# Softmax attention's stack transfers: projected rows laid dimension by dimension with the heads side by side

## The chip, the cores and the metric

The kernel runs on one core of one Trainium2 chip. The metric is the device time of one launch in microseconds (us); less is better. The median of the runs before is 2393.15 us.

## The reference

Sixteen sequences of 512 rows with 256 features pass through four residual blocks in turn: attention with a memory ("attention a"), a feed-forward block, softmax attention with rotary positions ("attention b"), and the feed-forward block again. The change is in attention b:

```python
q = jnp.einsum('kd,bsd->bsk', W_Q, in_features).reshape(B, S, H, d_k)   # 16 heads of 16 dimensions
k = jnp.einsum('kd,bsd->bsk', W_K, in_features).reshape(B, S, H, d_k)
q, k = _rope(q, THETA), _rope(k, THETA)      # mixes dimensions 2n and 2n+1 of a head
scores = jnp.einsum('bhqd,bhkd->bhqk', q, k) * scale
scores = jnp.where(causal[None, None], scores, -jnp.inf)
attn = jax.nn.softmax(scores, axis=-1)
out = jnp.einsum('bhqk,bhkd->bhqd', attn, v)
```

A score is a sum over the 16 dimensions of a head, so the order of the dimensions within a head may be chosen freely, if it is the same for q and k.

## The kernel before, in words

Four pieces of work, called lanes, run interleaved, each on its own sequence: lane 1 is attention a, lane 2 is attention b (`lane2`), F1 and F2 are the two feed-forward blocks. Every engine has its own program. On each engine the steps of the lanes are merged by `in_order` by hand-written marks (the table MARKS, L78): the step with the lowest mark is next, so each engine's order is fixed and an engine waits in place for a step that isn't ready. The 16 sequences pass through a start, a loop of 13 turns (`Fori`) that holds all four lanes, and an end. Steps are tied by semaphores alone.

Matrix products take float16 operands, with each float32 value split in a high and a low part. For attention b, lane 2 does this in each sequence:

- PB: TensorE projects q and k, 128 features (8 heads, "a half") at a time: q and k of half 0, then of half 1 (L1359). The features lie in the partitions by parity: partition r*64 + n holds feature 2n + r, so that the rotation pairs partitions n and n + 64. ScalarE copies the swapped halves (L868), VectorE and GpSimd apply cosine and sine (L1239, L709, L712), ScalarE makes the high part (L873, tile `sth`), VectorE the low part (L1244, L1248, tile `stl`). In the trace all these tiles have the name `place`.
- `stack` (L518), on the SP queue, step PB of SyncE's marks: the parts go to DRAM (`scratch`) and come back stacked, so that one product over 64 rows gives (high + low) times (high + low). For a half, four transfers write 64 partitions each to `scratch` (L531), in the natural order of the features. SP waits for their landing (L533). Then eight transfers read (L540): each fills 16 partitions (the 16 dimensions of a head) of `qst` or `kst` for 8 heads with 512 columns of float16, that is 128 KB. The fourfold stack has the rows q: high, high, low, low, and k: high, low, high, low.
- N(h), h from 0 to 15: TensorE waits for the landing of head h's half (`stacks_landed`, L1412), then computes head h's scores (`scores`, L1547, with the mask added by L1549), and VectorE takes their row maxima (L1256). The maxima are turned on TensorE (L1608) and go by small transfers within SBUF into rows 96 and 97 of `qst` (L571). NS(h) computes the scores again, transposed and shifted (L1561), ScalarE takes the exponentials (L897), PV, TP, OT and WO give the output.

Lane 1 has a `stack` of its own, with the same four writes a half, and sixteen reads of 64 KB a half (L545). Between the two stacks of lane 2, SP issues the load of lane 1's next sequence, `xa` (L552), as soon as `xa` was last used (L1060); VectorE's norm of it begins with L1024. The feed-forward blocks have UP (L1395 on TensorE, L788 and L791 on ScalarE, L649 on GpSimd) and DN (L1408). Near step N(0) of lane 2, TensorE's order is: UP steps of a feed-forward block, N(0), two more UP steps, the first of DN, N(1).

Before the lanes start there is a setup. SP loads the weights (L503), biases, the cosine and sine tables by parity (L509) and the memories (L514). VectorE waits for the weights (L952), scales and splits them; those of W_Q and W_K of attention b in `split_by_parity` (L960): 4 pieces of 128 columns a matrix, two instructions each (L967, L968). Every setup instruction of VectorE waits for the one before it (`link`).

## Time and profile before

| what | us |
|---|---|
| median of 3 runs | 2393.15 |
| lowest and highest run | 2391.18, 2405.67 |
| the profiled execution, its own time | 2384.41 |
| its span, first to last instruction | 2382.7 |

The rows further down are of the profiled execution. Its own time is 1.7 us over its span; it lies 8.7 us (0.4%) below the median. Times in the trace count from the span's start. Engines: PE is TensorE, PEld its weight loads, DVE VectorE, ACT ScalarE, POOL GpSimd, SP SyncE; a "q" behind one is its queue, where DMAs are issued and semaphores awaited. PEclk is the granted clock of TensorE as a share of 2.4 GHz. GB/s is what the core's 16 DMA engines moved in a stretch.

### The profile page before, as it was taken

The page shows a single profiled execution, that of the slowest core. Times are in us where ns is not written, and L with a number is a line of the kernel's source. Part 1 is how long each engine was busy: PE and PEld are TensorE (multiplying, and loading weights), DVE is VectorE, ACT ScalarE, POOL GpSimd, SP SyncE. Part 2 cuts the span into 40 slices and gives each one's busy share as a digit, 9 for nine tenths or more (in the row PEclk, how much of TensorE's full clock was granted, in tenths as well). Part 3 has the DMA queues.
Part 4 walks back from the last instruction along what each step waited for, and adds up shares of the span by engine and source line. Part 5 has one row for each costly group of instructions (what it writes and reads, how often), then busy time and mean ns, then how long its engine had stood idle before and what let it go on. Part 6 is the DMA issues. An engine that isn't in the chain of part 4 may idle for free. (4 is left out here: it accounts for less than half of the span.)

```text
span 2382.7 us, 53440 instructions
## 1 busy us (share of the span) xinstructions
PE 1908.6 (80%) x18306; PEld 1211.5 (51%) x18306; DVE 1604.3 (67%) x3874; ACT 1359.5 (57%) x2694; POOL 1140.0 (48%) x978
## 2 busy tenths in 40 slices
PE   0556798979888897979888797988889797888876
PEld 0334455545555554545555454555555455555443
DVE  6545776768676676868677685867667686866352
ACT  0324465756566575755666575655657575564644
POOL 0326355563635555472645546363555536363222
PEclk9668898989999998999999898999999899999999
DMA  3201414233050424224051423305142421404040
GB/s 92 54 21 42 75 42 63 64 55 73 13 93 24 63 64 63 64 30 91 8 90 38 63 64 53 74 11 90 29 63 64 63 64 25 91 13 63 1 63 10
DMA packets 125081, 126.63 MB, mean 53 GB/s; under 512 B 22800, under 2 KB 107920, under 8 KB 124816
## 3 DMA queue, kind: packets, MB, share of 16 engines
q1 hardware_dynamic: 116368, 114.58, 26.0%
q10 hardware_dynamic: 8448, 8.39, 1.1%
q8 instruction: 181, 2.97, 0.5%
q14 instruction: 84, 0.69, 0.1%
HBM read 80.43 MB, written 41.94 MB: 51 GB/s over the span
## 5 line engine op out<-in xcount | busy, mean ns | idle before, releaser
L1256 DVE TENSOR_REDUCE mxs<-bank 128x1 f32<-128x128 f32 (+3 forms) x1024 | 427.6, 480 | 167.2 <-PE bank L1549 166.5
L897 ACT ACTIVATE place<-bank 128x512 f32<-128x512 f32 (+1 forms) x768 | 348.7, 530 | 104.6 <-PE bank L1563 103.4
L659 POOL TENSOR_TENSOR place<-am,place 128x512 f16<-128x512 f32 x256 | 291.2, 1159 | 206.9 <-ACT place L803 206.9
L649 POOL TENSOR_TENSOR place<-place 128x512 f16<-128x512 f32 x256 | 300.6, 1182 | 139.9 <-ACT place L791 135.2
L1547 PE MATMUL bank<-kst,qst 96*128 96x128 f16 (+3 forms) x1024 | 258.3, 315 | 86.6 <-DMA kst<-scratch 62.9
L1408 PE MATMUL bank<-w2q,place 128*128 128x256 f16 x2048 | 248.4, 274 | 1.8 <-POOL place L649 1.0
L634 POOL TENSOR_TENSOR rstd<-ve,halfc 128x4 f32<-128x4 f32 x64 | 64.8, 1012 | 385.2 <-DVE ve L1031 385.2
L1561 PE MATMUL bank<-qst,kst 128*128 128x512 f16 (+3 forms) x1024 | 229.5, 301 | 14.9 <-DVE mxs L1256 6.7
L788 ACT ACTIVATE place<-bank,b1c 128x512 f32<-128x512 f32 x256 | 175.3, 685 | 108.4 <-PE bank L1395 88.9
L1549 PE MATMUL bank<-mask_qk,identb 128*128 128x128 bf16 x1024 | 223.2, 227 | 0.0
L687 POOL TENSOR_TENSOR place<-place 128x512 f16<-128x512 f32 x64 | 82.9, 1299 | 281.1 <-ACT place L827 260.0
L1408 PEld LDWEIGHTS bank<-w2q,place 128*128 128x128 f16 x2048 | 196.7, 98 | 36.0 <-issue 6.5
L1090 DVE SCALAR_TENSOR_TENSOR am<-bank,tri 128x512 f32<-128x512 f32 x256 | 167.3, 685 | 59.9 <-PE bank L1426 35.3
L803 ACT ACTIVATE place<-am 128x512 f16<-128x512 f32 x256 | 151.7, 628 | 93.8 <-DVE am L1090 93.8
L1395 PE MATMUL bank<-xh,w1q 128*128 128x512 f16 x512 | 168.8, 414 | 21.2 <-ACT place L788 15.2
L1547 PEld LDWEIGHTS bank<-kst,qst 96*128 96x128 f16 x1024 | 101.5, 100 | 164.6 <-DMA kst<-scratch 70.6
L1563 PE MATMUL bank<-mask_kq,identb 128*128 128x128 bf16 x1024 | 183.6, 219 | 0.0
L791 ACT ACTIVATE place<-place 128x512 f16<-128x512 f32 x256 | 161.3, 630 | 8.2
L1395 PE MATMUL bank<-xlo,w1q 128*128 128x512 f16 x512 | 165.2, 407 | 0.0
L1574 PE MATMUL bank<-place,vb 128*32 128x512 f32 (+3 forms) x2048 | 151.1, 435 | 3.2 <-ACT place L897 2.4
L666 POOL TENSOR_TENSOR place<-place 128x384 f32<-128x384 f32 x128 | 134.1, 1048 | 32.4 <-DVE place L1112 32.4
L1561 PEld LDWEIGHTS bank<-qst,kst 128*128 128x128 f16 x1024 | 101.0, 99 | 95.4 <-DVE mxs L1256 17.7
(162 smaller groups left out, 4000.5 us busy)
## 6 DMA issues: line engine op xcount, KB each, us to landing
scratch<-place SPq DMA_DIRECT2D x256, 128.0 KB, 2.4
qst<-scratch SPq DMA_DIRECT2D x256, 64.0 KB, 2.3
kst<-scratch SPq DMA_DIRECT2D x256, 64.0 KB, 2.3
qst<-scratch SPq DMA_DIRECT2D x128, 128.0 KB, 5.2
kst<-scratch SPq DMA_DIRECT2D x128, 128.0 KB, 5.8
xa<-x SPq DMA_DIRECT2D x16, 512.0 KB, 7.5
out<-xg ACTq DMA_DIRECT2D x16, 512.0 KB, 3.2
qst<-nmt SPq DMA_DIRECT2D x128, 4.0 KB, 1.8
```

The lines of the kernel that those rows point to most:

```text
L649: G.tensor_tensor(L.hl[:, m, :], L.hf[:, m % 2, :], L.hh[:, m, :], ALU.subtract).then_inc(s["hl"], 1)
L659: G.tensor_tensor(alp[:, n % 2, k, :], am[:, k, :], ahp[:, n % 2, k, :], ALU.subtract).then_inc(s["al"], 1)
L788: A.activation(L.hf[:, m % 2, :], bank_of(L, ("UP", m))[:, :], ACT.Relu, bias=b1c[:, m:m + 1]).then_inc(s["hf"], 1)
L897: A.activation(pf[h % SLOTS][:, S2_COL[k]:S2_COL[k] + S2_W[k]], bank_of(L2, ("S2", h, k))[:, 0:S2_W[k]], ACT.Exp, scale=D ** -0.5 / RS ** ...
L1090: V.scalar_tensor_tensor(am[:, k, :].rearrange("p (c s) -> p c s", c=NT), bank_of(L1, ("PR", n, k))[:, :].rearrange("p (c s) -> p c s", c= ...
L1256: V.tensor_reduce(mxs[:, g:g + 1], bank_of(L2, ("S1", n, k))[:, Q_AT[i]:Q_AT[i] + (i + 1) * P], AX, ALU.max).then_inc(s["mx"], 1)
L1395: ins = T.matmul(into[:, :], w1q[:, k, m * P:(m + 1) * P], a[:, k, :], start=(n == 0), stop=(n == 3))
L1408: ins = T.matmul(into[:, a * H:(a + 1) * H], part[:, m, cols], w2q[:, m, :], start=(m == 0 and part is L.hh), stop=(m == FT - 1 and part i ...
L1547: T.matmul(into[:, Q_AT[i]:Q_AT[i] + (i + 1) * P], L2.qst[0:STK, h, i * P:(i + 1) * P], L2.kst[0:STK, h, 0:(i + 1) * P], start=True, stop= ...
L1549: ins = T.matmul(into[:, Q_AT[i] + i * P:Q_AT[i] + (i + 1) * P], identb[:, :], mask_qk[:, :], start=False, stop=True, skip_group_check=True)
L1561: T.matmul(into[:, at:at + (NT - kt) * P], L2.kst[:, h, kt * P:(kt + 1) * P], L2.qst[:, h, kt * P:S], start=True, stop=True)
L1563: ins = T.matmul(into[:, at:at + P], identb[:, :], mask_kq[:, :], start=False, stop=True, skip_group_check=True)
```

## The change

The features of a half of attention b lie in the partitions in another order: partition r*64 + m*8 + h holds dimension 2m + r of head h, where it was dimension 2m + r at partition r*64 + h*8 + m. Read as d*8 + h, this gives 16 dimensions (the even ones first), each with its 8 heads side by side. The DRAM buffer of lane 2, `by_dim`, keeps this order, with the planes q and k apart, so that what fills a partition of `qst` or `kst` (8 heads of 512 columns, 8 KB) is one contiguous run. Four things follow:

- Writes (both lanes): two transfers a half of 128 partitions each, 256 KB, in place of four of 64 partitions, 128 KB. In lane 1 a partition's run stays 2 KB; in lane 2 it was 2 KB and becomes two of 1 KB (q and k go to different planes).
- Reads (lane 2): six a half in place of eight: two of 32 partitions fill `kst` (high and low together, 256 KB), four of 16 partitions fill `qst` (128 KB). The bytes that land are the same, 1 MB a half. Lane 1's reads are unchanged.
- Setup: the tables of cosine and sine are first copied from DRAM to DRAM in the new order, by four transfers at the head of SP's queue, and SP waits for them before it loads the tables. `split_by_parity` has twice as many instructions of half the size (64 columns), 32 in place of 16.
- The semaphores' counts follow (`bounced`, `LANDED`, `DVE_SETUP`). The marks, and so the order of steps on each engine, are the same.

```diff
--- before.py
+++ after.py
@@ -54,7 +54,7 @@
 
 
 NORM = dict(bn=4, tick=1, mv=4, ve=1, rstd=1, shift=1, xn=4, xt=2, xh=2, xl=2)
-OUTS = dict(v=2, vh=2, sh=4, sl=4, bounced=128, wo=2, xres=2)
+OUTS = dict(v=2, vh=2, sh=4, sl=4, bounced=64, wo=2, xres=2)
 FFN = dict(up=8, hf=8, hh=8, hl=8, xb=1, dn=2, xffn=2)
 PER1 = dict(
     NORM, **OUTS, xin=16, proj=4, e=4, r=4, sq=4, sk=3, skt=3,
@@ -67,7 +67,7 @@
     pv=4, ev=4, tp=4, prec=4, tb=4, ot=2, oh=2, ol=2,
 )
 PERF = dict(NORM, **FFN, store=16)
-LANDED = {1: 2 * 4 * 2 * 16, 2: 2 * 4 * 16}
+LANDED = {1: 2 * 4 * 2 * 16, 2: 6 * 16}
 
 CUT = 7
 
@@ -455,14 +455,16 @@
         prec = sb("prec", [P, 2, 16])
 
 
-        scratch = nc.dram_tensor("scratch", (2, KH, 2, P, 2, S), F16, kind="Internal").ap()
+        by_head = nc.dram_tensor("by_head", (KH, 2, P, 2, S), F16, kind="Internal").ap()
+        by_dim = nc.dram_tensor("by_dim", (KH, 2, 2, P, S), F16, kind="Internal").ap()
+        tables = nc.dram_tensor("tables", (2, 2, PAIR, S), F32, kind="Internal").ap()
         for L in (L1, L2):
             L.landed = [sem(f"landed{half}_{L.n}") for half in range(KH)]
-            L.scratch = scratch[L.n - 1]
 
         w_in = sem("w_in")
         f_in = sem("f_in")
         c_in = sem("c_in")
+        t_in = sem("t_in")
         g_in = sem("g_in")
         m_in = sem("m_in")
         pool_const = sem("pool_const")
@@ -470,7 +472,7 @@
         act_setup = sem("act_setup")
         pe_setup = sem("pe_setup")
         primed = sem("primed")
-        DVE_SETUP = 50
+        DVE_SETUP = 66
         block = ctx.enter_context(nc.Block())
 
         x_in, x_out = (t.rearrange("(b j p) f -> b p j f", b=B, p=P) for t in (x, out))
@@ -492,6 +494,10 @@
         @block.sync
         def _(sp):
             at1, at2 = marks(1, "sync"), marks(2, "sync")
+            for n, of in enumerate((cos, sin)):
+                for r in range(2):
+                    sp.dma_start(tables[n, r].rearrange("(m h) s -> m h s", h=HH8),
+                                 of.rearrange("(h m r) s -> r m h s", r=2, h=HH8)[r]).then_inc(t_in, 16)
             sp.dma_start(gates[:, 0, :], gate.broadcast_to([P, NH])).then_inc(g_in, 16)
             sp.dma_start(f_stage[:, 0:NFW].rearrange("p (k f) -> p k f", k=KH),
                          w1t.rearrange("(k p) f -> p k f", p=P)).then_inc(f_in, 16)
@@ -504,10 +510,10 @@
                              wv[:, n]).then_inc(w_in, 16)
             sp.dma_start(b1c[:, :], b1t).then_inc(c_in, 16)
             sp.dma_start(b2bc[:, :], b2.broadcast_to([P, H])).then_inc(c_in, 16)
-            for table, of in ((cost, cos), (sint, sin)):
+            sp.wait_ge(t_in, 64)
+            for n, table in enumerate((cost, sint)):
                 for r in range(2):
-                    sp.dma_start(table[r * PAIR:(r + 1) * PAIR, :],
-                                 of.rearrange("(n r) s -> r n s", r=2)[r]).then_inc(c_in, 16)
+                    sp.dma_start(table[r * PAIR:(r + 1) * PAIR, :], tables[n, r]).then_inc(c_in, 16)
             sp.wait_ge(pool_const, 1)
             for half in range(KH):
                 for h in range(HH8):
@@ -524,22 +530,26 @@
                 sp.wait_ge(s["sh"], due(L, "sh", t, 2 * half + 2))
                 sp.wait_ge(s["sl"], due(L, "sl", t, 2 * half + 2))
                 for part, src in enumerate((L.sth, L.stl)):
-                    for r in range(2):
-                        rows = slice(r * PAIR, (r + 1) * PAIR)
-                        to = L.scratch[half, part]
-                        to = to[rows] if L is L1 else to.rearrange("(n r) w s -> r n w s", r=2)[r]
-                        sp.dma_start(to, src[rows, 2 * half:2 * half + 2, :]).then_inc(s["bounced"], 16)
-
-                sp.wait_ge(s["bounced"], due(L, "bounced", t, 64 * (half + 1)))
+                    to = by_head[half, part] if L is L1 else by_dim[half, :, part].rearrange("w p s -> p w s")
+                    sp.dma_start(to, src[:, 2 * half:2 * half + 2, :]).then_inc(s["bounced"], 16)
+
+                sp.wait_ge(s["bounced"], due(L, "bounced", t, 32 * (half + 1)))
                 heads = slice(half * HH8, (half + 1) * HH8)
                 pairs = slice(half * HH8 // 2, (half + 1) * HH8 // 2)
+                if L is L2:
+                    for k in range(2):
+                        sp.dma_start(L.kst[2 * k * D:2 * (k + 1) * D, heads, :].rearrange("p h s -> p (h s)"),
+                                     by_dim[half, 1].rearrange("a (d h) s -> (a d) (h s)", h=HH8)
+                                     ).then_inc(L.landed[half], 16)
+                        for j in range(2):
+                            row = (2 * k + j) * D
+                            sp.dma_start(L.qst[row:row + D, heads, :].rearrange("p h s -> p (h s)"),
+                                         by_dim[half, 0, k].rearrange("(d h) s -> d (h s)", h=HH8)
+                                         ).then_inc(L.landed[half], 16)
+                    return
                 for k, (q_part, k_part) in enumerate(((0, 0), (0, 1), (1, 0), (1, 1))):
                     for dst, part, which in ((L.qst, q_part, 0), (L.kst, k_part, 1)):
-                        rows = L.scratch[half, part, :, which, :]
-                        if L is L2:
-                            sp.dma_start(dst[k * D:(k + 1) * D, heads, :],
-                                         rows.rearrange("(h d) s -> d h s", d=D)).then_inc(L.landed[half], 16)
-                            continue
+                        rows = by_head[half, part, :, which, :]
                         for r in range(2):
                             to = slice(r * PARTS + k * D, r * PARTS + (k + 1) * D)
                             sp.dma_start(dst[to, pairs, :], rows.rearrange("(g r d) s -> r d g s", r=2, d=D)[r]
@@ -961,11 +971,13 @@
                 for n in range(KH * H // P):
                     row, col = divmod(n * P, H)
                     at = mat % BQ * KH * H + n * P
-                    of = w_stage[mat // BQ][:, at:at + P].rearrange("p (n r) -> p r n", r=2)
-                    hi = wh[:, mat, row, col:col + P].rearrange("p (r n) -> p r n", r=2)
-                    lo = wl[:, mat, row, col:col + P].rearrange("p (r n) -> p r n", r=2)
-                    link(V.tensor_scalar(hi, of, WS, None, ALU.mult))
-                    link(V.scalar_tensor_tensor(lo, of, WS, hi, ALU.mult, ALU.subtract))
+                    for r in range(2):
+                        of = w_stage[mat // BQ][:, at:at + P].rearrange("p (h m r) -> p r m h", r=2, h=HH8)[:, r]
+                        to = slice(col + r * PAIR, col + (r + 1) * PAIR)
+                        hi = wh[:, mat, row, to].rearrange("p (m h) -> p m h", h=HH8)
+                        lo = wl[:, mat, row, to].rearrange("p (m h) -> p m h", h=HH8)
+                        link(V.tensor_scalar(hi, of, WS, None, ALU.mult))
+                        link(V.scalar_tensor_tensor(lo, of, WS, hi, ALU.mult, ALU.subtract))
 
             split_weights(0, BQ)
             split_by_parity(BQ)
```

## Rows read from the trace of the kernel before

**Rows 1.** The page: span and busy time of TensorE.

```profile
span 2382.7 us, 53440 instructions
PE 1908.6 (80%) x18306; PEld 1211.5 (51%) x18306; DVE 1604.3 (67%) x3874; ACT 1359.5 (57%) x2694; POOL 1140.0 (48%) x978
```

**Rows 2.** The chain that ended last, at sequence 14's stack: start, duration, what.

```profile
2145.18 1.41 DVE place L1244
...
2148.49 2.37 DMA scratch<-place
...
2154.07 7.66 DMA kst<-scratch
2162.17 0.32 PE bank L1547
```

**Rows 3.** Waits, PE's and SP's: total us, times, longest.

```profile
PE bank L1547 <- DMA kst<-scratch: 62.9, 16, 7.9
...
PE bank L1426 <- DMA kst<-scratch: 6.7, 2, 5.0
```
```profile
SPq L540 <- DMA scratch<-place: 106.3, 32, 6.5
```

**Rows 4.** TensorE's timeline at N(0) of four sequences: start, duration, [idle before].

```profile
262.80 0.29 PE L1547 MATMUL bank<-kst,qst 96*128 96x128 f16 x1 [7.88 <-DMA kst<-scratch]
...
528.91 0.29 PE L1547 MATMUL bank<-kst,qst 96*128 96x128 f16 x1 [2.23 <-DMA kst<-scratch]
...
1210.06 0.29 PE L1547 MATMUL bank<-kst,qst 96*128 96x128 f16 x1 [4.04 <-DMA kst<-scratch]
...
1211.52 1.06 PE L1395 MATMUL bank<-xh,w1q 128*128 128x512 f16 x2
...
1620.10 0.29 PE L1547 MATMUL bank<-kst,qst 96*128 96x128 f16 x1 [4.76 <-DMA kst<-scratch]
```

**Rows 5.** Stretches around N(0): length, busy by engine, PEclk, DMA share, GB/s.

```profile
528.70:532.10 3.40, 3.19 (x13) 1.59 (x14) 2.33 (x7) 0.23 (x1) 1.37 (x2) 0.51 0.66 230
1208.00:1214.80 6.80, 4.74 (x16) 2.17 (x17) 3.54 (x14) 1.56 (x3) 1.41 (x2) 0.50 0.80 191
...
1222.00:1275.00 53.00, 49.96 (x509) 31.78 (x509) 47.62 (x114) 35.54 (x76) 18.81 (x16) 1.00 0.27 72
```

**Rows 6.** SP's timeline, lane 2's stack of half 0.

```profile
1194.40 2.42 SPq L531 DMA_DIRECT2D scratch<-place  x4
1198.60 0.31 SPq L540 DMA_DIRECT2D qst<-scratch  x1
...
1203.27 0.40 SPq L552 DMA_DIRECT2D xa<-x  x1
```

**Rows 7.** Stretches with one kind of transfer in flight; the last column is GB/s.

```profile
1195.50:1198.20 2.70, 2.01 (x13) 1.05 (x11) 1.56 (x4) 0.60 (x2) 2.55 (x3) 1.00 0.88 194
1200.50:1209.00 8.50, 4.72 (x29) 2.37 (x26) 3.54 (x4) 7.03 (x12) 7.64 (x7) 0.94 1.17 114
1209.50:1210.50 1.00, 0.44 (x3) 0.34 (x4) 0.00 (x0) 0.00 (x0) 0.00 (x0) 0.50 1.12 354
...
4.00:5.00 1.00, 0.00 (x0) 0.00 (x0) 0.79 (x1) 0.00 (x0) 0.00 (x0) 1.00 1.03 410
```

**Rows 8.** ACT, POOL and DVE around that N(0), each from its timeline.

```profile
1207.63 0.63 ACT L791 ACTIVATE place<-place 128x512 f16<-128x512 f32 x1
```
```profile
1207.10 2.39 POOL L649 TENSOR_TENSOR place<-place 128x512 f16<-128x512 f32 x2 [0.28 <-ACT place L791]
```
```profile
1216.52 1.68 DVE L1256 TENSOR_REDUCE mxs<-bank 128x1 f32<-128x128 f32 x4 [1.98 <-PE bank L1549]
```

**Rows 9.** VectorE's timeline in the setup.

```profile
15.70 1.23 DVE L957 TENSOR_SCALAR wh<-qst 128x2048 f16<-128x2048 f32 x1 [10.90 <-DMA kst<-wall]
...
19.28 0.23 DVE L967 TENSOR_SCALAR wh<-kst 128x128 f16<-128x128 f32 x1
19.54 0.29 DVE L968 SCALAR_TENSOR_TENSOR wl<-kst,wh 128x128 f16<-128x128 f32 x1
```

## The prediction, made before the changed kernel was run

> **What bounds the kernel now.** The page comes first: TensorE is busy for 80% of the span, more than any other engine [rows 1]. An order fixed by hand adds to that the waits that stand in TensorE's own order, so the next view is the list of its waits. One of the largest is L1547, the first scores of lane 2, which waits for the landing of `kst`: 62.9 us in 16 waits, one in each sequence [rows 3]. The chain that ended last runs through the same place: the low parts (L1244), SP's writes to `scratch`, their landing, the reads, their landing, L1547 [rows 2]. So this is no idle time beside the bound. TensorE's timeline gives the single waits: 7.88 us in the first sequence, and in the three later ones shown 2.23, 4.04 and 4.76 us; the mean of the 15 after the first is (62.9 - 7.9)/15 = 3.7 us [rows 3, 4].
>
> The wait costs a second time. In the stretch 1208.0 to 1214.8 the granted clock is 0.50, that is 1.2 GHz, while from 1222 to 1275, where TensorE is hardly ever idle, it is 1.00, 2.4 GHz [rows 5]. TensorE did nothing for 4.04 us before the fall, and ran 4.74 us of work after it at half speed. In an early sequence with a wait of 2.23 us, 3.19 us of work ran so [rows 4, 5]. Between these two lie about 4 us a sequence, of which half, 2 us, would be saved at full clock.
>
> **How the path to N(0) is made up.** SP's timeline: writes issued from 1194.40, first read issued at 1198.60, N(0) starts at 1210.06 [rows 4, 6]. That is 4.2 us for the writes and 11.5 us for the reads. The stretches with one kind of transfer in flight show what sets each. Reads into 16 partitions go at 114 GB/s; writes from 64 partitions at 194; the load of `xa` into 128 partitions at 354, and its runs are 1 KB, as those of the reads are [rows 7]. Runs of 4 KB into 128 partitions (w1t and w2t, in the setup) reach 410 [rows 7]. So the rate follows how many partitions a transfer touches, and the length of a run little: 1 KB to 4 KB gives 16%, 16 to 128 partitions gives a factor of 3.
>
> **Writes.** A half is 0.52 MB: 2.7 us at 194 GB/s. With 128 partitions and runs of 1 KB I take the rate of `xa`, 354: 1.5 us. Two issues of 0.6 us (2.42/4, [rows 6]) keep ahead of that. Gain 1.2 us; bounds 0 (they stay at 194) and 1.4 (410). The `xa` row is the nearest, being the same run and partitions in the other direction.
>
> **Reads.** A half is 1.05 MB: 9.2 us at 114 GB/s. Afterwards half of the bytes (`kst`) go into 32 partitions, half (`qst`) still into 16. No row has 32 partitions; it lies between 16 (114) and 64 (194). I take 210, near the row of 64 and somewhat above, since those writes were issued one by one every 0.6 us and 128 KB in 0.6 us is 218: 2.5 us for `kst`, 4.6 us for `qst`, together 7.1, gain 2.1 us. Bounds: 0 (`kst` at 114 too) and, if the long runs lift both to 194 or more, 9.2 - 5.4 = 3.8 us. Six issues in place of eight save nothing, as data, not issue, is the limit: the eight are issued before 1203.27 [rows 6], 7 us before N(0) starts.
>
> A rule bears on this. The Trainium skill, in "SBUF — State Buffer", section "Door 1: The DMA port swizzle", says that a transfer's rate is set by the number of SBUF's 16 ports that its partitions reach: 16 partitions reach 4 (about 109 GB/s), 32 reach 8 (about 218), and 64 no more than 32. The trace agrees where it can: 114 for 16, 194 for 64 [rows 7]. By the rule's figures, as an estimate, the reads would take 2.4 + 4.8 = 7.2 us. It speaks against the "longer" in this change: a run of 8 KB gives nothing by it, and `qst` keeps its rate.
>
> N(0)'s data so lands 1.2 + 2.1 = 3.3 us earlier.
>
> **What that removes.** TensorE's readiness for N(0) doesn't depend on these transfers. The first wait, 7.88 us, keeps 4.6. The others lie between 2.2 and 4.8; less 3.3 us, those over 3.3 leave up to 1.5 us, on average 0.4 to 0.5. So 3.2 us x 15 + 3.3 = 51 us of idle time go. With waits of a few tenths to 1.5 us, I expect the clock to stay up: 2 us x 15 = 30 us. (In 1222 to 1275, with 3 us of idle time in 53, it did [rows 5].)
>
> **What is late next.** While TensorE waited (1206.0 to 1210.06), ScalarE finished its UP steps at 1208.3 and GpSimd its own at 1209.5 [rows 8]. Now two more UP steps come some 3 us sooner, and their banks and buffers with less slack; the first needs what ScalarE released before 1207. VectorE takes N(1)'s maxima at 1216.52 after a wait of 1.98 us for TensorE [rows 8], so it has room for the clock's 2 us but little over it. From 1222 on it is busy 47.6 of 53 us [rows 5]: it follows at the new time, but catches up nothing. The load of `xa` is issued at 1203.27, when `xa` is free, unchanged [rows 6]; its data stand in the queue behind the reads, and come earlier with them. I charge 0.8 us a sequence, 12 us in all; bounds 0 and 5 us a sequence (the rival below). Half 1's stack and lane 1's are not waited for in the loop, so their gain is nothing; in the start, lane 1's scores wait twice for their stacks (6.7 us, [rows 3]), which gives 1.2 us twice, 2.4.
>
> **What the setup costs.** Four copies at the head of SP's queue delay the weights, for which VectorE waits until 15.70 [rows 9]. Four issues are 2.4 us; their 0.5 MB is hidden in this if it moves at 354 GB/s, and would cost 2.2 us more at 114. I take 2.4. The wait for the copies is over long before the tables are issued, behind ten loads. The split: 8 pairs at 0.59 us (19.28 to 19.87, of which the two rows shown are 0.52 busy) become 16 pairs of half the size, each between 0.29 (no cost) and 0.59 (4.7 us more). Most of so small an instruction is fixed, so 0.48: 3.0 us more. VectorE's setup is one chain and ends last, so all 5.4 us count.
>
> **The sum.** -51 - 30 + 12 - 2.4 + 5.4 = -66 us. The profiled execution's own time, 2384.4, would become 2318. The median of the runs shown lies 8.7 us above it, so I forecast 2393.1 - 66 = 2327 us, 2.8% less.
>
> **Rivals.**
> - A. The reads gain more: the long runs lift `qst` as well. Data land 5.0 us earlier (1.2 + 3.8), every wait but the first is gone: 55 + 5 = 60 us, clock 30, charge of 12, setup 5.4, lane 1 2.4: -75, and with no charge -87. Time 2306 to 2318, say 2312. For it: nothing shows what the 16-partition reads wait for beyond their partitions. Against: 410 against 354 for longer runs [rows 7].
> - B. The reads gain nothing: 32 partitions filled in one transfer go no faster than two of 16. Then 1.2 us x 16 = 19 us of idle time, the clock falls still, setup 3 net: -16, 2377 us. That the transfers still move in runs of 1 KB, so that the change does not do what it says, would leave `kst` its 32 partitions, and is my forecast unless this rival holds as well.
> - C. The wait goes, another takes its place: ScalarE, GpSimd or VectorE holds N(1), UP or DN so that half of the 81 us come back, -40 + 3 = -37: 2356 us. For it: the row of POOL ends 3.5 us after TensorE went idle. Against: VectorE's wait of 1.98 us for TensorE [rows 8].
> - D. Slower. A 16-partition transfer is now 16 runs of 8 KB, one for each DMA engine, where it was 128 runs. If so few and long runs keep an engine from overlapping one with the next, the rate falls. It decides from where the reads take over 9.2 + 1.2 = 10.4 us, 101 GB/s. With a quarter of the rate lost (86 GB/s, 12.2 us) N(0) comes 1.8 us later: 29 us + 3 = +32, 2425 us. Against: 4 KB runs are the fastest seen [rows 7].
>
> **Chances.** Forecast 0.50, A 0.20, B 0.15, C 0.10, D 0.05. Apart from D all are below the time before; about 1% (24 us) is what a measurement can tell from no change. The forecast, A and C lie beyond it and make 0.80 together, a little of B's range reaches it: faster 0.81; same 0.14, from B and the mild end of D; slower 0.05. The range runs from A with no charge (2306), with a little for an unseen gain, to a weak B: 2300 to 2380.
>
> **What would show it.** L1547's wait for `kst` on TensorE falls from 62.9 us to some 10 to 12, most of it in the first sequence. From the first write's issue to the first read's it is about 3 us (4.2 before), and from there to the landing about 9 (11.5 before). The rate in the reads swings between some 110 and 200 GB/s with the kind of transfer. After N(0) the granted clock is 1.00, and L1395's pairs take 0.59 us where they took 1.06 [rows 4]. The setup ends 5 us later. It is wrong if the reads' total stays at 9 us of data, if the clock still falls after N(0), or if L1408, L1395 or the scores of N(1) to N(3) show new waits of over 1 us.

## The result, and the profile after

| what | us |
|---|---|
| before, median of 4 runs (lowest, highest) | 2392.3 (2391.2, 2405.7) |
| after, median of 4 runs (lowest, highest) | 2300.7 (2298.3, 2303.0) |
| ratio, with its 95% interval | 0.9605 [0.9569, 0.9641] |
| the profiled execution of after, its own time, its span | 2303.0, 2301.3 |

By the medians the change gains 91.6 us, 3.8%; the ratio compares means and gives 4.0%. The forecast was 66 us and 2327, with a range of 2300 to 2380. The median after lies at its lowest end, and 0.9605 of the 2393.15 us on record is 2298.6, just below it: more was gained than the forecast allowed for. The page of after, span and engines, then the queue that fetches instructions (packets, MB, share):

```profile
span 2301.3 us, 53268 instructions
...
PE 1904.0 (83%) x18306; PEld 1207.5 (52%) x18306; DVE 1617.6 (70%) x3890; ACT 1361.3 (59%) x2694; POOL 1140.6 (50%) x978
...
q14 instruction: 23, 0.19, 0.0%
```

The same queue on the page of before:

```profile
q14 instruction: 84, 0.69, 0.1%
```

TensorE is busy 4.6 us less than before [rows 1], its idle time falls from 474.1 to 397.3 us (span less busy). So almost all of the profiled difference is idle time, though the forecast had 30 us of it in the clock. TensorE's waits after, total, times and longest; the new number of L1547 is L1559, that of L1443 is L1455:

```profile
PE bank L1455 <- DVE am L1102: 46.1, 26, 3.2
...
PE bank L1407 <- ACT place L798: 14.5, 33, 2.2
PE bank L1559 <- DMA qst<-by_dim: 7.9, 6, 4.0
```

and the row of before that answers to the first:

```profile
PE bank L1443 <- DVE am L1090: 78.6, 26, 4.9
```

The wait for the stack falls from 62.9 us [rows 3] to 7.9 (forecast: 10 to 12). Of the 7.9, 3.98 are in the first sequence, and the next five wait 0.45 to 1.21 us each; after those, the data land 0.1 to 1.9 us before N(0) starts. But a second wait falls as well, by 32.5 us, of which the prediction had nothing: lane 1's products that wait for VectorE's `am`.

**At N(0)**, it goes by the plan. SP's timeline, then TensorE's:

```profile
1292.94 0.91 SPq L534 DMA_DIRECT2D by_dim<-place  x2
1295.88 0.33 SPq L541 DMA_DIRECT2D kst<-by_dim  x1
...
1303.24 0.40 SPq L562 DMA_DIRECT2D xa<-x  x1
```
```profile
1305.84 0.22 PE L1559 MATMUL bank<-kst,qst 96*128 96x128 f16 x1
...
1306.62 0.59 PE L1407 MATMUL bank<-xh,w1q 128*128 128x512 f16 x2
...
1309.08 1.27 PE L1420 MATMUL bank<-w2q,place 128*128 128x256 f16 x10 [0.40 <-ACT place L798]
```

First write to first read is 2.94 us where it was 4.20 [rows 6]. N(0) starts without idle time before it, 9.96 us after the first read's issue (11.46 before). The pair L1407 takes 0.59 us, where L1395 took 1.06 at half clock [rows 4]. The windows of after (length, busy by engine, PEclk, DMA share, GB/s), for the writes, the reads, and the reads' end with the load of `xa`:

```profile
1293.80:1295.40 1.60, 1.60 (x16) 1.31 (x14) 1.46 (x3) 0.60 (x2) 1.46 (x3) 1.00 0.95 323
1297.50:1303.20 5.70, 5.62 (x38) 3.38 (x36) 2.29 (x5) 4.77 (x9) 5.55 (x5) 1.00 0.90 164
1303.50:1310.20 6.70, 5.87 (x35) 2.91 (x36) 4.79 (x15) 6.37 (x11) 5.55 (x6) 1.00 0.59 179
```

Writes go at 323 GB/s (194 before), reads at 164 (114 before, [rows 7]), and the clock is full. The reads' packets run from 1296.8 to 1303.1: 1.05 MB in 6.3 us. This is one of the faster stacks. Over half 0 of all 16 sequences the data take 6.2 to 8.2 us, in the median 6.9. From the issue of the first read to the last landing it is 8.8 us in the median (8.1 to 9.9), and was 11.5 (10.9 to 12.2) before.

**At the end of a turn of the loop** VectorE had a pause between two instructions, with nothing it waited for ("issue"). There are 12 such pauses in before, 32.0 us in all; this one is 2.60. Before, then after:

```profile
1307.51 0.28 DVE L1121 TENSOR_TENSOR xlo<-bank,xh 128x128 f16<-128x128 f32 x1
1310.39 1.41 DVE L1024 BATCH_NORM_STATS2 stats<-xb 128x6 f32<-128x256 f32 x4 [2.60 <-issue]
```
```profile
1272.30 0.28 DVE L1133 TENSOR_TENSOR xlo<-bank,xh 128x128 f16<-128x128 f32 x1
1272.70 1.40 DVE L1036 BATCH_NORM_STATS2 stats<-xb 128x6 f32<-128x256 f32 x4
```

The pause is gone in every turn. TensorE's `L1443` waited right behind it, and the clock stood at half. TensorE's row of before, then the half-clock stretch at that place before and after:

```profile
1313.80 0.63 PE L1443 MATMUL bank<-bmh,place 64*128 64x272 f16 x4 [4.65 <-DVE am L1090]
```
```profile
1310.40:1317.20 6.80, 3.40 (x36) 2.74 (x36) 5.15 (x23) 2.08 (x4) 2.03 (x2) 0.50 0.01 2
```
```profile
1274.50:1284.70 10.20, 6.78 (x46) 4.30 (x47) 7.30 (x23) 4.62 (x9) 4.29 (x4) 0.51 0.01 2
```

This also says why the busy time hardly fell: half clock at N(0) is gone except in the first sequence, but the stretch at the loop's end is longer and holds 6.78 us of work in place of 3.40. Over the span the half-clock time goes from 344 to 295 us.

**The setup** costs more than forecast. VectorE after:

```profile
21.92 1.23 DVE L967 TENSOR_SCALAR wh<-qst 128x2048 f16<-128x2048 f32 x1 [17.12 <-DMA kst<-wall]
...
25.51 0.21 DVE L979 TENSOR_SCALAR wh<-kst 128x64 f16<-128x64 f32 x1
25.75 0.26 DVE L980 SCALAR_TENSOR_TENSOR wl<-kst,wh 128x64 f16<-128x64 f32 x1
26.05 0.21 DVE L979 TENSOR_SCALAR wh<-kst 128x64 f16<-128x64 f32 x1
```

The weights come 6.2 us later (21.92 against 15.70, [rows 9]); a pair takes 0.54 us (25.51 to 26.05), 16 of them 8.6, against 8 of 0.59, 4.7.

### The profile page after: what moved, and what is told of

Its sections match the earlier page's. It is cut to its first block and busy times, and to the rows that moved or that the text cites. A ratio compares the mean times of both kernels' runs of the same rounds, so it can differ in the third digit from the quotient of the medians.

```text
span 2301.3 us, 53268 instructions
## 1 busy us (share of the span) xinstructions
PE 1904.0 (83%) x18306; PEld 1207.5 (52%) x18306; DVE 1617.6 (70%) x3890; ACT 1361.3 (59%) x2694; POOL 1140.6 (50%) x978
## 5 line engine op out<-in xcount | busy, mean ns | idle before, releaser
L1559 PE MATMUL bank<-kst,qst 96*128 96x128 f16 (+3 forms) x1024 | 250.8, 306 | 33.5 <-DVE mxs L1268 16.9
L1561 PE MATMUL bank<-mask_qk,identb 128*128 128x128 bf16 x1024 | 218.2, 222 | 0.0
L1407 PE MATMUL bank<-xh,w1q 128*128 128x512 f16 x512 | 157.8, 391 | 21.5 <-ACT place L798 14.5
L1407 PE MATMUL bank<-xlo,w1q 128*128 128x512 f16 x512 | 156.1, 387 | 0.0
L1559 PEld LDWEIGHTS bank<-kst,qst 96*128 96x128 f16 x1024 | 99.6, 98 | 107.5 <-DVE mxs L1268 37.1
L818 ACT ACTIVATE xh<-bank 128x128 f16<-128x128 f32 x128 | 35.6, 278 | 201.5 <-PE bank L1482 199.5
```

What stands on the lines that cost most here:

```text
L1407: ins = T.matmul(into[:, :], w1q[:, k, m * P:(m + 1) * P], a[:, k, :], start=(n == 0), stop=(n == 3))
L1559: T.matmul(into[:, Q_AT[i]:Q_AT[i] + (i + 1) * P], L2.qst[0:STK, h, i * P:(i + 1) * P], L2.kst[0:STK, h, 0:(i + 1) * P], start=True, stop= ...
L1561: ins = T.matmul(into[:, Q_AT[i] + i * P:Q_AT[i] + (i + 1) * P], identb[:, :], mask_qk[:, :], start=False, stop=True, skip_group_check=True)
```

## The experiments

Two theories of the 91.6 us stand against each other. F: some 30 us are no effect of the transfers; the 16 added setup instructions shifted VectorE's code behind them, and with it the pause at the loop's end. The rival: all comes from the transfers, the pause went because the phase of the loop changed. On the transfers' side, theory P says that the number of partitions sets the rate, and the length of a run does not.

### e1 and e2: the code's place alone

e1 is the kernel before with 16 instructions more in VectorE's setup, e2 the kernel after with 112 more. They touch no transfer.

```diff
-        DVE_SETUP = 50
+        DVE_SETUP = 66
...
+            for _ in range(16):
+                link(V.memset(L1.tick[:, :], 0.0))
             split_weights(0, BQ)
```

> The kernel before with 16 more tiny instructions in VectorE's setup (they write a tile that is written again later), nothing else. Theory F (placement of code): in the kernel before VectorE stands 2.6 us at the end of every turn of the loop, with nothing in the profile that it waits for, and queue 14 fetches instructions in every turn; the changed kernel has neither, since its 16 more setup instructions moved the loop's code. By F this kernel loses the 2.6 us too: a period of 133.5 to 134 us in place of 136.3, queue 14 at some 25 packets in place of 84, time 2360 to 2368 us. Rival (the stall went because the stacks land earlier, or because SP issues less): period 136.3, 84 packets, time 2394 us, 2 us of setup more.

Measured: 2365.3 us, ratio 0.9849 [0.982, 0.9878], against 2397.7 for before, measured beside it: 32 us gained by adding work. e1's instruction queue, its waits and VectorE's loop end (a turn of its own):

```profile
q14 instruction: 24, 0.20, 0.0%
```
```profile
PE bank L1549 <- DMA kst<-scratch: 65.2, 16, 7.4
...
PE bank L1445 <- DVE am L1092: 44.8, 26, 3.2
```
```profile
1163.85 0.28 DVE L1123 TENSOR_TENSOR xlo<-bank,xh 128x128 f16<-128x128 f32 x1
1164.25 1.40 DVE L1026 BATCH_NORM_STATS2 stats<-xb 128x6 f32<-128x256 f32 x4
```

The wait for the stack stays (65.2), that for `am` falls to the value of after. The stretch at half clock at the loop's end grows as it does in after, with the transfers untouched, and TensorE's busy time rises from 1908.6 to 1925.1 us: the clock takes back part of what the pause gave.

```profile
1300.30:1310.50 10.20, 7.70 (x48) 4.63 (x49) 6.45 (x21) 5.47 (x11) 3.72 (x5) 0.50 0.01 2
```

> The changed kernel with 112 more tiny instructions in VectorE's setup. A packet of queue 14 is 8 KB, so if an instruction is 64 bytes (an estimate), 16 + 112 = 128 bring the loop's code back to where it lay in the kernel before, relative to such a block. Theory F: the stall of about 2.6 us a turn and the fetches in each turn come back, the period goes from 129.7 to about 132.3 us, time 2300 + 34 + 10 (setup) = 2344 us. Rival (the stall went for another reason): period 129.7, time 2310 us, only the setup longer.

Measured: 2343.3 us, 0.9768 [0.9743, 0.9793]; the pause is back, with the packets and the wait:

```profile
q14 instruction: 84, 0.69, 0.1%
```
```profile
PE bank L1457 <- DVE am L1104: 76.8, 24, 4.9
```
```profile
1301.98 0.28 DVE L1135 TENSOR_TENSOR xlo<-bank,xh 128x128 f16<-128x128 f32 x1
1304.90 1.40 DVE L1038 BATCH_NORM_STATS2 stats<-xb 128x6 f32<-128x256 f32 x4 [2.65 <-issue]
```

Of its 42.6 us over after, 15.7 are the added instructions (N(0) of the first sequence comes so much later) and 27 the loop. The pause can be taken away and put back without touching a transfer: the rival falls.

The trace also shows what stands in the pause. This is the instruction queue's row for the stretch 1308.20 to 1309.00 of before, inside the pause that begins at 1307.79:

```profile
q14 instruction: 1, 0.01, 2.5%
```

The packet starts 0.72 us after the pause begins and has ended 1.56 us before VectorE's next instruction. All 12 pauses of before hold one such packet, and so do the 12 of e2 and the 12 of e7 (0.7 to 1.0 us into the pause). From one pause to the next the queue has 5 packets; 12 turns of 5 are the 60 that go or come. In e1 from 500 to 2100 us and in after from 500 to 2040, that is in the loop, it has none.

### e3 and e4: partitions or runs

e3 reads `kst` in 16-partition transfers again (eight reads a half), in the order `qst`, `kst` as before; all else is as after. e4 keeps the six reads and pads a row of `by_dim`, so that its runs are 1 KB.

```diff
# e3
-                        sp.dma_start(L.kst[2 * k * D:2 * (k + 1) * D, heads, :].rearrange("p h s -> p (h s)"),
-                                     by_dim[half, 1].rearrange("a (d h) s -> (a d) (h s)", h=HH8)
...
+                            for dst, which, part in ((L.qst, 0, k), (L.kst, 1, j)):
+                                sp.dma_start(dst[row:row + D, heads, :].rearrange("p h s -> p (h s)"),
+                                             by_dim[half, which, part].rearrange("(d h) s -> d (h s)", h=HH8)
# e4
-        by_dim = nc.dram_tensor("by_dim", (KH, 2, 2, P, S), F16, kind="Internal").ap()
+        by_dim = nc.dram_tensor("by_dim", (KH, 2, 2, P, S + 64), F16, kind="Internal").ap()[:, :, :, :, 0:S]
...
```

> The changed kernel with the reads of kst cut in two, so that all eight fill 16 partitions, still with runs of 8 KB, in the order q, k, q, k as before. Theory P (the rate is set by the partitions that a transfer reaches): 114 GB/s again, from the first read's issue to the landing about 11 us where the changed kernel has under 8.5, a wait of 2 to 3 us at N(0) in every sequence, the clock at half after N(0), time 2300 + 45 to 60 = 2345 to 2360 us. Theory L (long runs made the reads faster): landing after some 8 us, no wait at N(0) in the loop, time 2300 to 2306 us.

> The changed kernel with each row of 512 columns padded in DRAM by 64 columns, so that the same six reads into the same 32 and 16 partitions move in runs of 1 KB and not of 8 KB. Theory P: as the changed kernel, data of the reads in 6 to 7.2 us, no wait at N(0) in the loop, 2300 us plus or minus 4. Theory L: back to 9 us of data, a wait of 1 to 2 us at N(0), 2315 to 2345 us.

Measured: e3 2318.1 us, 0.9671 [0.9632, 0.9709]; e4 2305.5, 0.9613 [0.9596, 0.963]. The reads of e3, then of e4:

```profile
1314.00:1321.00 7.00, 6.21 (x40) 3.51 (x39) 3.54 (x4) 6.36 (x12) 6.59 (x5) 1.00 1.00 113
```
```profile
1170.20:1176.50 6.30, 5.71 (x39) 3.48 (x38) 2.90 (x5) 5.30 (x10) 6.15 (x5) 1.00 1.05 164
```

P holds in this: runs of 8 KB into 16 partitions go at 113 GB/s, no faster than runs of 1 KB did before, and runs of 1 KB go at 164 in the reads of after. e3 can't say whether the 32 partitions or the order does it, for e3 also brings back the order of before, in which `qst` and `kst` are filled for the same 16 partitions one behind the other; that is e7's question. The longer runs bring the last landing 0.8 us sooner (8.8 us after the first read's issue in after, 9.7 in e4), but little of that reaches the time: at most the 5 us between after and e4, which were measured apart and whose intervals overlap. Rival D ends here. e3's last landing comes 11.1 us after the first read's issue, as expected, but its time is only 17 us over after's, where 45 to 60 were expected. Its waits at N(0) came back, 29.5 us in all, but short, and in 13 of 16 sequences the clock stayed up:

```profile
1323.10 0.23 PE L1557 MATMUL bank<-kst,qst 96*128 96x128 f16 x1 [1.24 <-DMA kst<-by_dim]
...
1323.89 0.59 PE L1405 MATMUL bank<-xh,w1q 128*128 128x512 f16 x2
```

### e5 and e8: four writes again, alone and with e3

```diff
                 for part, src in enumerate((L.sth, L.stl)):
...
+                    for r in range(2):
+                        rows = slice(r * PAIR, (r + 1) * PAIR)
...
+                        sp.dma_start(to, src[rows, 2 * half:2 * half + 2, :]).then_inc(s["bounced"], 16)
```

> The changed kernel with the writes of both lanes cut in two again, four of 64 partitions. Theory P: from the first write's issue to the first read's 4.2 us again, where it is 2.9. The data for N(0) land 1.3 us later; in the loop of the changed kernel they land some 2 us before TensorE is ready, so nothing of this shows but in the first sequence (1.3 us) and for lane 1's first stacks: 2301 to 2305 us. Rival (the writes are worth their 1.3 us in every sequence): 2300 + 20 = 2320 us.

> The changed kernel with both kinds of transfer cut as they were, four writes of 64 partitions and eight reads of 16: what is left of the change is the order of the rows, runs of 8 KB, the longer setup, and the place of VectorE's code. Theory P: transfers as in the kernel before (4.2 us and some 11 us), so the time of the kernel before without VectorE's stall (2365 us) plus the setup's 10: 2370 to 2378 us. Rival (long runs still give part): 2335 to 2360 us. From e3, whose landing took 11.1 to 11.4 us with two writes, 2345 to 2355 could also come out if the 1.3 us of the writes count fully (1.3 x 2 x 15 with the clock).

Measured: e5 2321.0 us, 0.9685 [0.9654, 0.9717]; e8 2372.0, 0.9911 [0.988, 0.9943], the 2370 to 2378 of its theory P. In e5 the writes take 4.48 us to the first read, and N(0) waits in every sequence:

```profile
1305.63 2.67 SPq L536 DMA_DIRECT2D by_dim<-place  x4
1310.11 0.33 SPq L543 DMA_DIRECT2D kst<-by_dim  x1
```
```profile
PE bank L1561 <- DMA qst<-by_dim: 27.8, 16, 6.1
```

Theory P of the expectation, 2301 to 2305 us, is wrong here. The writes are 1.5 us later and the reads' last landing 0.5 us more (9.3 us after the first issue, 8.8 in after), 2.0 in all; after has 0.1 to 1.9 us to spare in ten of its sequences and none in the other six. Undoing the writes costs 20 us, the 32 partitions 17, but both 71. e8 shows why, in its waits and at N(0):

```profile
PE bank L1559 <- DMA kst<-by_dim: 49.6, 16, 7.5
```
```profile
1339.92 0.29 PE L1559 MATMUL bank<-kst,qst 96*128 96x128 f16 x1 [2.89 <-DMA kst<-by_dim]
...
1341.39 1.06 PE L1407 MATMUL bank<-xh,w1q 128*128 128x512 f16 x2
```

Here the wait is 2.89 us and the clock is at half afterwards: N(0) to N(1) takes 5.3 us (5.3 to 6.7 before from the second sequence on, 4.35 after, 3.70 in e3). The five kernels side by side; the second column is how much later than in after the last landing of half 0 comes, counted from the first write's issue (medians):

| kernel | landing later | waits at N(0) | sequences at half clock after N(0) | time over after |
|---|---|---|---|---|
| after | | 7.9 | 1 of 16 | |
| e4 | 0.8 | 6.5 | 1 | 5 |
| e5 | 2.0 | 27.8 | 3 | 20 |
| e3 | 2.2 | 29.5 | 3 | 17 |
| e8 | 3.8 | 49.6 | 16 | 71 |

The waits simply add: 19.9 us in e5 and 21.6 in e3 are 41.5, and e8 has 41.7. What does not add is TensorE's busy time, 1904.0 us in after, 1906.6 in e5, 1900.9 in e3 and 1921.7 in e8, and that is the clock. The length of a wait does not settle it by itself. Over all runs, N(0) was followed by full clock after every wait of up to 1.70 us and by half clock after every one of 3.1 us and more, but between 1.8 and 3.0 us both occur; here is one of e3 at full clock:

```profile
932.63 0.23 PE L1557 MATMUL bank<-kst,qst 96*128 96x128 f16 x1 [2.55 <-DMA kst<-by_dim]
...
933.43 0.59 PE L1405 MATMUL bank<-xh,w1q 128*128 128x512 f16 x2
```

What else decides between these two is open. In that region a change of 1 to 2 us can pay more than its length.

### e7 and e11: the old transfers in another order

In the stretch shown, after's reads were faster (6.3 us) than the two rates of the prediction give (7.1); over all sequences they were not by much (6.9). In after the two reads of `qst` that follow each other fill different partitions; before, and in e3, `qst` and `kst` were filled for the same 16 one behind the other. Theory O: neighbours that fill different partitions overlap. e7 is the kernel before with lane 2's eight reads in the order of rows 0-15, 16-31, 0-15, 16-31, 32-47, 48-63, 32-47, 48-63. e11 adds e1's 16 instructions.

```diff
+                turns = [(L.qst, 0, 0, 0), (L.kst, 0, 1, 0), (L.qst, 1, 0, 0), (L.kst, 1, 1, 1),
+                         (L.qst, 2, 0, 1), (L.kst, 2, 1, 0), (L.qst, 3, 0, 1), (L.kst, 3, 1, 1)]
+                if L is L2:
+                    turns = [turns[n] for n in (0, 3, 1, 2, 4, 7, 5, 6)]
```

> The kernel before with the eight reads of a half of lane 2 in another order alone: rows 0-15, 16-31, 0-15, 16-31, 32-47, 48-63, 32-47, 48-63, in place of each range twice in a row. Theory P in its simple form (one transfer after the other, each at the rate of its own 16 partitions): no change, 114 GB/s, 2393 to 2398 us. Theory O (neighbouring transfers overlap, and together reach the rate of all the partitions that they touch; that is why the changed kernel's reads take 6 us and not 7.1): 150 GB/s or more, landing 2 us sooner, 2393 - 30 to 40 = 2355 to 2363 us.

> The kernel before with the two smallest edits found so far: the 16 tiny setup instructions (e1, -32 us) and the other order of the reads (e7, -29 us). If the two are independent: 2395 - 61 = 2334 us, waits at N(0) of 25 to 40 us, queue 14 at some 24 packets. If one eats the other (an earlier turn of the loop's end brings TensorE to N(0) sooner, and it waits longer there): 2345 to 2360 us.

Measured: e7 2364.2 us, 0.9885 [0.9852, 0.9917]; e11 2335.8, 0.9772 [0.9754, 0.979]. e7's reads:

```profile
1325.30:1333.00 7.70, 6.79 (x42) 3.66 (x40) 3.54 (x4) 6.97 (x13) 7.21 (x6) 1.00 1.13 156
```

156 GB/s against 114, but not all of it is the reads: 156 GB/s over 7.7 us are 1.20 MB, and the reads are 1.05, so the load of `xa` behind them is already in it. The landings are free of that. In this stack the eight reads land 1.01 us apart on average where they landed 1.19 apart before, that is 130 GB/s against 110, and over all sequences the last landing comes 10.3 us after the first issue (9.5 to 10.9) in place of 11.5. So the order of the same eight transfers, with the same bytes and the same partitions each, changes their rate by some 18%. That neighbours on different partitions overlap is a reading of this. It is 1.2 of the 2.7 us that after gains; eight reads of 16 partitions in this order with after's layout were not run, so what the 32-partition transfers add by themselves stays open. N(0)'s waits sum to 37.0 us; one of them, with the pair behind it at full clock:

```profile
1334.12 0.23 PE L1551 MATMUL bank<-kst,qst 96*128 96x128 f16 x1 [1.25 <-DMA qst<-scratch]
...
1334.92 0.59 PE L1399 MATMUL bank<-xh,w1q 128*128 128x512 f16 x2
```

Order is worth 30 us by itself, and 55 together with the placement of the code (30 + 32 would be 62): two small edits give 60% of the whole change, without a new layout.

### e6: the copies behind the weights; e9 and e10: the load of xa moved

e6 is after with the four copies of the tables issued behind the loads of the weights. In e9 (on e5) and e10 (on e6) a mark of SyncE goes from 28 to 29, so that `xa` is loaded behind the stack of half 1: does this load, issued right behind the reads, stretch their end?

```diff
# e6: the loop over (cos, sin) with its dma_start(tables[n, r]...) moved from the head of SP's program
             sp.dma_start(w_stage[n // BQ]...
...
+            for n, of in enumerate((cos, sin)):
...
             sp.dma_start(b1c[:, :], b1t).then_inc(c_in, 16)
# e9, e10
-            "T": [28],
+            "T": [29],
```

> The changed kernel with the four copies of the cosine and sine tables issued after the eight loads of weights, not before all loads. If the 6.2 us by which VectorE's first weights are late come from these copies (they move at some 160 GB/s, and the weights stand behind them), the weights are there at 15.7 us again and the kernel takes 2300.7 - 6 = 2294 to 2296 us. Rival (the setup's end is set by another load, or by the tables themselves, now late): 2300 us, and VectorE waits for the memories or primed instead.

> e5 (four writes) with the load of xa issued behind the stack of half 1 and not between the two stacks. e5 took 20 us more than the changed kernel where 1.3 us later landings with 2 us to spare should have cost nothing. Theory X: the load of xa, issued at a fixed time, now meets the tail of the later reads of half 0 and stretches it; then the waits at N(0) fall from 27.8 us to under 12 here, though VectorE may wait for xa instead before the maxima of N(1). Theory S: there never were 2 us to spare, the data of the changed kernel land just in time, and every later landing counts at once; then the waits at N(0) stay at 20 to 30 us.

> e6 (table copies after the weights) with the load of xa behind the stack of half 1. By both theories nothing is gained at N(0), where e6 hardly waits. The load is issued some 5 us later than in e6 (after half 1's reads), VectorE takes its norm between the maxima of N(0) and N(1), so VectorE waits for it, N(1) and all behind it come 3 to 5 us later in each turn: 2293 + 45 to 70 = 2340 to 2360 us. If VectorE has that much to spare: 2290 to 2296 us.

Measured: e6 2293.2 us, 0.9578 [0.9558, 0.9597], the best of all; its highest run, 2295.1, is below the lowest of after, though the two were measured apart and the intervals of their ratios overlap. Its weights are there 5.6 us sooner than after's:

```profile
16.37 1.23 DVE L967 TENSOR_SCALAR wh<-qst 128x2048 f16<-128x2048 f32 x1 [11.58 <-DMA kst<-wall]
```

e9 is 2449.1 us, 1.0243 [1.0225, 1.0262], e10 2421.2, 1.0122 [1.0101, 1.0143], both above before. In e9 the waits of N(0) for the stack are 12.4 us in sum against 27.8 in e5, and the last landing comes 8.8 us after the first read's issue, not 9.3, so `xa` does slow the end of the reads. But the norm now waits for `xa`:

```profile
DVE stats L1038 <- DMA xa<-x: 152.7, 15, 11.5
...
PE bank L1561 <- DVE mxs L1270: 147.7, 24, 10.8
```

I had expected a loss of 3 to 5 us a turn in e10; it is 128 us over e6, some 8 to 10 a turn. Most of it goes the same way: in e10 VectorE's norm waits 136.9 us for `xa` in 15 waits of up to 10.2, and behind it TensorE's wait for VectorE's maxima grows from 16.9 us in e6 to 129.3.

## Why the prediction was right, and where it was not

**The step that failed** is the one on the split of the weights, "so 0.48: 3.0 us more": it counted the added instructions of VectorE by their own time and put what they do to the code behind them at nothing. The runs show 32 us there (e1). The setup's other term, "I take 2.4", is the second: it was 6.2. With these two in place the forecast's -66 becomes -66 - 32 + 5 = -93, and the medians give 91.6.

**What bounds the kernel, and what the wait costs: right in the main.** L1547's wait went, and nothing of more than 1 us took its place at N(0). The step "what is late next" is there too: ScalarE holds TensorE between N(0) and N(1) for 0.65 us in sum (4.35 us from one to the other, 3.70 in e3), where the charge was 0.8 a sequence. e8 against after gives the part of the number of transfers by itself, with the new layout in both: 71 us by the medians, and the terms of the forecast without the setup (-51 - 30 + 12 - 2.4) make 71. That they meet so closely is partly luck. The profiled executions of the two are 59 us apart: idle time falls by 41.0 (forecast 51 - 12 + 2.4 = 41.4), busy time by 17.7 (forecast 30). Inside the idle part, the waits at N(0) fall by 41.7 where 51 stood, lane 1's in the start by 3.5 where 2.4 stood, and what is late next costs 4 and not 12. The clock's term was sized too large in this pair: behind N(0), e8 loses less to half clock than before did (N(0) to N(1) 5.3 us, 5.7 in the median before). From before to after the busy time falls by 4.6 us only, since the end of the pause lengthens half clock at the loop's end (16.5 us more busy time in e1). The reading behind the term was not exact either: in the stretch shown the clock fell at 1208.0, and TensorE had then been idle for 2.0 us, not 4.04. The 12 us between 59 and 71 lie within the spread of e8's runs (2361.7 to 2381.0) and are not settled.

**Writes: right.** 4.20 to 2.94 us, gain 1.26 for 1.2.

**Reads: right in size, incomplete in kind.** The data take 6.9 us in the median for 7.1 forecast, and 9.2 in e3, where every transfer fills 16 partitions again, for the 9.2 of before in the forecast. To the last landing the gain is 2.7 us, for 2.1. Runs play a small part (e4: 0.8 us of landing). What the step to "together 7.1" lacked is the order: it took transfers as following one another, each with a rate of its own, and by that e7 would have gained nothing. e7 gains 1.2 us of landing. The Trainium skill's port rule ("SBUF — State Buffer", "Door 1: The DMA port swizzle"), which the prediction weighed, gave 7.2 us, and the trace agrees with 6.9. It tells what one transfer can reach and nothing of order; by what means order changes the rate no run here shows.

**Of the rivals.** A came nearest in time (2312), for a wrong reason: the long runs did not lift `qst` (e4). By A the reads would have gained 3.8 us; they gained 2.7. B, C and D are refuted by the windows, by the waits and by e3's 8 KB runs at 113 GB/s.

**Setup: right in sign, half the size.** VectorE's first norm begins at 66.23 us where it began at 56.05, 10.2 later and not 5.4. The step "Four issues are 2.4 us; their 0.5 MB is hidden in this" failed: weights were 6.2 late. It priced a copy from DRAM to DRAM by `xa`'s 354 GB/s; in the stretch 2.50 to 6.00, with the copies in flight, the DMA engines moved 134 GB/s. The prediction's own upper bound (2.4 + 2.2) fell short as well. The split cost 4.0 for 3.0. e6 wins back what the copies cost.

**What the prediction did not have.** Its step on the split ("so 0.48: 3.0 us more") counted the added instructions by their time alone, and took the code behind them as unmoved. That left out 32 us: the pause at the loop's end, which the trace of before shows, as a row with "issue" for a releaser, and with 84 packets of the instruction queue. The pause is 2.6 us of the turn, and behind it TensorE's wait of 4.65 us. That the change took the pause away is luck: no one had aimed at it, and with 112 more instructions (e2) it would have stayed.

**The sum.** From 2392 to 2398 us, the measured time of before, the pause's end takes 32 (e1: 2365.3), and between e8 (2372.0) and after (2300.7) lie 71. The 7 us between e1 and e8 are the rest, but they are not the setup alone, which is 10 us longer: e8's turn is 133.2 us and e1's 134.4, with the stack's data landing 15.5 us after the first write in both. So the new layout gives a little back by a way that was not followed up, and the two kernels were measured apart, where before itself moved by 3.5 us. The forecast added 8.7 us to get from the profiled execution of before to its median. That is not part of the miss: the gain is 91.6 us by the medians and 81.4 by the profiled executions (2384.4 to 2303.0), against 66 in both ways of counting.

What remains open is which placements of VectorE's code have the pause. Before, e2 and e7 have it (84 packets), the other ten kernels have not (23 or 24), and the rule between them is open. The time at which the loop begins is not it: the first N(0) starts at 262.8 us in before, with the pause, and at 263.3 in e6, without. That the pause is the fetch of instructions rests on the packet that stands in every one of the 36 pauses of these three kernels, and on the loop without packets where there is no pause; what VectorE does in the 1.4 to 1.6 us between the packet's end and its next instruction, no record shows.

## What to carry to other kernels

Look for idle time with "issue" as releaser at a loop's end, beside the packets of the instruction queue: here 16 more instructions ahead of the loop gave 32 us, a third of the whole gain, and any edit that changes the number of instructions moves this cost, so a control with padding is needed before an edit's gain is believed. Let transfers that follow each other fill different partitions, in one transfer or by their order, before lengthening runs. A wait costs more where the clock falls behind it, so measure two savings together as well as singly; and issue bulk copies that are needed late behind the loads that a chain waits for.

## What the runs showed of the hardware that was not expected

- Sixteen more memsets ahead of a loop took 32 us off (ratio 0.985), 112 others put 27 us into it; each time 60 or 61 packets of the instruction queue went or came, and one packet stands in each of the pauses of 2.6 to 2.9 us.
- The same eight 128 KB reads landed 1.19 us apart and, in another order, 1.01 (110 and 130 GB/s).
- Copies from DRAM to DRAM, 0.5 MB in four transfers, showed 134 GB/s in their stretch and held back the loads behind them by 6.2 us.
- TensorE's clock after a wait: with idle times of 1.24 and 1.25 us (e3, e7) the pairs behind took 0.59 us, with 2.89 us (e8) 1.06, but with 2.55 us in e3 0.59 again.
- Two delays of 2.0 and 2.2 us cost 20 and 17 us alone and 71 together; the waits added, the busy time did not.
